# Cross-attention block on one core: the planner's order of TensorE, ScalarE and VectorE is replaced by written strings

## What is computed

```
q = (layer_norm(x) * g + b) @ Wq + bq        # 16 heads of 16
k, v = ctx @ Wk + bk, ctx @ Wv + bv
attn = softmax(q @ k.T / 4)                  # 512 x 1601 for each head
y = x + (attn @ v) @ Wo + bo
out = y + silu(layer_norm(y) @ W1 + b1) @ W2 + b2      # FF = 1024
```

## Time and profile before

| what | us |
|---|---|
| median of three runs | 3663.59 |
| the profiled execution | 3659.6 |
| its span | 3657.8 |
| prologue, until the first quarter's scores | 96 |
| batch 0 / each of batches 1 to 14 / batch 15 | 202.2 / 222.3 / 192.1 |
| busy in a middle batch: TensorE / VectorE / ScalarE / GpSimd | 216.5 / 153.4 / 140.2 / 58.7 |

### The profile page before, as it was taken

One profiled execution on the slowest core, in us unless ns is written; L12 is line 12 of the kernel. 1 busy time (PEld: TensorE's weight loads), 2 busy tenths in 40 slices (PEclk: granted clock), 3 DMA queues, 4 the chain that ended last, 5 costly groups with the idle time before them and its releaser, 6 DMA issues.

```text
span 3657.8 us, 52477 instructions
## 1 busy us (share of the span) xinstructions
PE 3495.7 (96%) x19620; PEld 1552.4 (42%) x19620; DVE 2474.9 (68%) x4580; ACT 2243.8 (61%) x2979; POOL 950.3 (26%) x1340
## 2 busy tenths in 40 slices
PE   6899999999999999999999999999999999999997
PEld 2333444444444444443444444444444444434434
DVE  6767667676676767667676676766767676676761
ACT  2566666666666665666656666566666656666564
POOL 5122223121231322323222241212313223132202
PEclk8999999999999999999999999999999999999999
DMA  4223212132221222212232121321213222122200
GB/s 97 60 40 63 40 33 46 34 66 42 36 49 32 59 42 52 41 30 52 42 66 40 29 48 35 66 43 33 50 32 61 43 44 49 30 53 42 43 7 12
DMA packets 121535, 162.96 MB, mean 45 GB/s; under 512 B 37040, under 2 KB 102592, under 8 KB 118208
## 3 DMA queue, kind: packets, MB, share of 16 engines
q1 hardware_dynamic: 120896, 159.40, 22.2%
q10 hardware_dynamic: 384, 0.20, 0.0%
HBM read 46.43 MB, written 8.39 MB: 15 GB/s over the span
## 4 chain that ended last, share of the span: by engine, by line
PE 81%; DVE 12%; ACT 3%; issue 2%; DMA 1%; SPq 0%; POOL 0%; ACTq 0%; DVEq 0%
PE o_ps L1197 20%; PE rows_ps L1163 19%; PE scores L1178 14%; DVE chunk_max L974 8%; PE side L1131 6%; PE side L1128 6%; PE side L1117 5%; PE side L1109 5%; ACT probs L821 2%; PE side L1113 1%; PE side L1121 1%; DVE stats L852 1%; DVE resid L879 1%; PE side L1100 1%; ACT ctxT L738 1%
## 5 line engine op out<-in xcount | busy, mean ns | idle before, releaser
L974 DVE TENSOR_REDUCE chunk_max<-rows_ps 128x1 f32<-128x512 f32 (+1 forms) x3328 | 2117.2, 666 | 1049.8 <-PE rows_ps L1163 1041.5
L821 ACT ACTIVATE probs<-scores 128x1024 f32<-128x1024 f32 (+1 forms) x1664 | 1676.9, 1024 | 1135.3 <-PE scores L1178 1128.3
L1163 PE MATMUL rows_ps<-k_stack,q_stack 96*128 96x512 bf16 (+1 forms) x4096 | 1215.7, 338 | 83.9 <-DVE chunk_max L974 52.4
L1178 PE MATMUL scores<-q_stack,k_stack 99*128 99x512 bf16 (+1 forms) x3328 | 1036.5, 379 | 7.2 <-DMA q_stack<-shift_parts 4.2
L1197 PE MATMUL o_ps<-probs,v_sb 128*32 128x512 f32 x6656 | 886.3, 605 | 0.4 <-ACT probs L821 0.4
L1163 PEld LDWEIGHTS rows_ps<-k_stack,q_stack 96*128 96x128 bf16 x4096 | 332.0, 97 | 1169.9 <-DVE chunk_max L974 960.9
L1178 PEld LDWEIGHTS scores<-q_stack,k_stack 99*128 99x128 bf16 (+1 forms) x3328 | 324.8, 100 | 303.7 <-issue 42.0
L585 POOL TENSOR_TENSOR rest<-whole,k_parts 128x512 f32<-128x512 f32 x124 | 117.1, 944 | 962.8 <-ACT k_parts L766 928.3
L1128 PE MATMUL side<-hT,w_sb 128*128 128x256 f32 x968 | 258.6, 379 | 0.0
L1197 PEld LDWEIGHTS o_ps<-probs,v_sb 128*32 128x32 f32 x6656 | 130.8, 108 | 294.3 <-issue 220.4
L1131 PE MATMUL side<-w_sb,ffT 128*128 128x256 f32 x960 | 244.9, 381 | 0.6
(11 more groups left out here) (126 smaller groups left out, 2054.0 us busy)
## 6 DMA issues: line engine op xcount, KB each, us to landing
k_stack<-k_parts SPq DMA_DIRECT2D x768, 50.0 KB, 2.2
k_stack<-k_stack SPq DMA_DIRECT2D x192, 200.1 KB, 5.6
ctx_nat<-in_ctx SPq DMA_DIRECT2D x47, 512.0 KB, 4.0
q_stack<-q_stack SPq DMA_DIRECT2D x192, 64.0 KB, 3.4
q_stack<-q_parts SPq DMA_DIRECT2D x756, 16.0 KB, 1.8
x_nat<-in_x SPq DMA_DIRECT2D x16, 512.0 KB, 6.1
resid<-in_x SPq DMA_DIRECT2D x32, 256.0 KB, 2.7
out<-resid SPq DMA_DIRECT2D x32, 256.0 KB, 2.5
```

Source lines behind the costliest of these rows:

```text
L821: nc.scalar.activation(probs[0:rows, (q + t) % 2, 2 * LQ * pair:2 * LQ * (pair + 1)], scores[0:rows, 2 * LQ * pair:2 * LQ * (pair + 1)], A ...
L974: nc.vector.tensor_reduce(dst, src, AX.X, ALU.max).then_inc(rows_read, 1)
L1163: last = nc.tensor.matmul(rows_ps[:, m % 2, d0:d0 + w], q_stack[s][0:STACK, h, P * t:P * (t + 1)], k_stack[s][0:STACK, h, k0:k0 + w], star ...
L1178: ins = nc.tensor.matmul(scores[0:keys_in(t), LQ * j:LQ * (j + 1)], k_stack[s][:, h, P * t:P * t + keys_in(t)], q_stack[s][:, h, :], start ...
```

## The change

The tables and `plan` are removed. `BOTH` lists only the sequence of side steps of each quarter (the same steps in the same quarters and sequence), and three tables of strings set the order: TENSOR (s, m, d, p as above), SCALAR (e an exponential, r the read of a side step, c the copy of `o_ps`), VECTOR (m a maxima read, i inversion, n negation, x and b moments, a the addition of wo, y of w2, g `finish_silu`). In the first and the last batch the letters of missing steps are skipped. The reads of the maxima, the exponentials and all waits are the same code as before. The first twelve slots of the opening quarter do two maxima each. "pp" is new: two PV tiles one after the other.

The turn's matmul gets all 128 columns: `neg_parts` is widened with zeros, and ScalarE still copies 12 partitions. For k and q ScalarE reads the bank once into `whole`, waits for that, and copies the first part from `whole` (semaphore `first_parts` tells GpSimd). For w1 it reads each half once, waits, and takes one tanh over 512 columns from `ffT` (semaphore `tanh_made` tells VectorE).

```diff
+TENSOR = (
+    "spmssmdsmdddmssmdddmdsmpsmmddddsmssmddddmsmpddmmssddddmddmpmmsddmsssmdmdmssssmppssmsmsddssmmpmmssssm"
+    "pmssmddddmssmssmpmmsddmsmddmssssppmmssddddmssmpmmddmsmsssmddmpm",
+    "ssmpdmdddssmssmddddmsmsddddpsdsdmmddpmssmddddmssmssmpmddmddssmssmdpdmmssdddmmsssdsmpmmpmssmdmsmdmsmp"
+    "mmdmdsmmsssdmmdmssmssdmdpmsddddsmpssddddmmpddddssmmssdmssmdssmmppmmss",
+    "dssdmdddmpmmdddsssmsmdddddmsmddsdssmmppmssmdssddmmddssdddmmppddmssssmdmddmdmssssmmddddmmssppmmssddmd"
+    "dddmmssssdddmmdddppmmssddmddssmmssddddmpmssmssddmmddpsssmsmddmssmddsmmpddddsmmspsmm",
+    "dmdmmssssdmmdssmpmmdsmsdmmpdsdmmssspmmssdmsmsssdmmppmmsssdmsdmssmddsmsmppmmsssdsmmdssddmmppssmmssddm"
+    "ddmdsddmssmspmmddddsmmdddddsssmmpmddddssssmmpmssmssmpmm",
+)
+SCALAR = (
+    "ceereereeereeeeereeeeeereeeereeeer",
+    "ecrerereerereererreeereerereererererereeeree",
+    "ecreeereeeerreereereeeeeeereereeerree",
+    "reerceerreeeereeeereeeereeeeeereeee",
+)
+VECTOR = (
+    "mmmmmmmimmmmmmimmmmmmmmmambmbbmmmmmmmmmmmmmmmmnmammmmmmmmbmbmbmg",
+    "mmmmimmxmmmmmmmxmmmmxmmimmmmmmmmmmmmmmmmmmmmmnmmmmgmmmmmmmm",
+    "mmmmmmmmmmmmmmmmmmmmmmmgmmigmmmmmmimmmmymmmmmnmmmmmmgmmmmgmm",
+    "mmmmmmmmmimmmmmmmmmimmmmmmmmmmmgmmgmmmmmmmmnmmmymmmmmmmmmm",
+)
...
-        neg_parts = sb("neg_parts", [P, QT, PARTS, 4], BF16)
+        neg_parts = sb("neg_parts", [P, QT, P // 4, 4], BF16)
...
-                    ins = nc.tensor.matmul(side[0:4 * PARTS, P * i:P * (i + 1)],
+                    ins = nc.tensor.matmul(side[:, P * i:P * (i + 1)],
...
-                    nc.scalar.activation(whole[:, n % 2, 0:w], src[:, 0:w], ACT.Identity, bias=bias, scale=scale)
-                    last = nc.scalar.activation(parts[:, 0, off:off + w], src[:, 0:w], ACT.Identity, bias=bias,
-                                                scale=scale)
+                    nc.scalar.activation(whole[:, n % 2, 0:w], src[:, 0:w], ACT.Identity, bias=bias, scale=scale)\
+                        .then_inc(side_read, 1)
+
+                    act.wait_ge(side_read, step_value(start, k))
+                    nc.scalar.copy(parts[:, 0, off:off + w], whole[:, n % 2, 0:w]).then_inc(first_parts, 1)
+                    return
...
+                    for half in range(2):
+                        m = 2 * m2 + half
+                        last = nc.scalar.activation(ffT[:, m, :], src[:, QH * half:QH * (half + 1)], ACT.Identity,
+                                                    bias=half_b1[:, m:m + 1], scale=0.5)
+                    last.then_inc(side_read, 1)
+
+                    act.wait_ge(side_read, step_value(start, k))
...
-                    last = halves_step(src, kind, arg, ffT, tanh_sb, hT)
+                    nc.scalar.activation(tanh_sb[:, :], ffT[:, 2 * m2:2 * m2 + 2, :].rearrange("p m q -> p (m q)"),
+                                         ACT.Tanh).then_inc(tanh_made, 1)
```

More of the change, by code:

```diff
@@ L73, in tiles_in @@
     return range(4 * c, min(4 * c + 4, KT))
[L78 to L84, removed]
+FINISHING = ("wo", "h", "w1", "w2")
@@ new lines, with kept @@
+SCALAR = (
[8 more added lines that the diff above has]
+    "mmmmmmmmmmmmmmmmmmmmmmmgmmigmmmmmmimmmmymmmmmnmmmmmmgmmmmgmm",
+    "mmmmmmmmmimmmmmmmmmmimmmmmmmmmmmgmmgmmmmmmmmnmmymmmmmmmmmm",
+)
+def kept(q, keep):
+    return [step for step in BOTH[q] if keep(step[0])]
@@ L104 @@
+FIRST = tuple(kept(q, lambda kind: kind not in FINISHING) for q in range(4))
+LAST_BATCH = (BOTH[0],) + tuple(kept(q, lambda kind: kind in FINISHING + ("turn",)) for q in (1, 2)) \
+    + (kept(3, lambda kind: kind in FINISHING),)
 PER_BATCH = sum(map(len, BOTH))
@@ L145, in products, with side_products, chosen @@
     return [(i, j) for i in range(first) for j in range(second)]
-def products_at(steps, u):
+def side_products(q, steps):
     found = []
[L151 to L155, removed]
-    return found
+    for step in BOTH[q]:
+        todo = products(*step)
+        for n, product in enumerate(todo):
+            found.append((steps.index(step),) + step + (product, n, n == len(todo) - 1) if step in steps else None)
+    return found
+def chosen(q, steps, kinds):
+    return [(steps.index(step),) + step if step in steps else None for step in BOTH[q] if step[0] in kinds]
 M_ROWS = QT * 4
@@ L184, in maxima @@
     return b + (q + ahead) // 4, (q + ahead) % 4, m
[L188 to L212, removed]
 def wait(eng, sem, value):
@@ L671, in quarter @@
             def quarter(b, q, start, steps):
-                kinds = [step[2:] for step in steps]
+                kinds = steps
                 ahead, s = PREPARED[q]
                 if q == 3:
-                    splits(b + ahead, s, start, steps)
+                    splits(b + ahead, s, steps)
                 if q > 0:
@@ L807, in quarter @@
                 ahead, s = PREPARED[q]
[L808 to L811, removed]
+                unit, reads = iter(range(UNITS)), iter(chosen(q, steps, ("v", "ctx", "k", "q", "x", "turn", "h", "w1")))
+                for what in SCALAR[q]:
+                    if what == "c":
                         if q > 0:
                             copy_group(b, q - 1)
-                        elif not (isinstance(b, int) and b == 0):
+                        elif b > 0:
                             copy_group(b - 1, 3)
[L817 to L828, removed]
+                    elif what == "r":
+                        read = next(reads)
+                        if read:
+                            k, kind, arg = read
+                            if kind in FINISHING:
+                                side_step(b - 1, None, start, k, kind, arg)
+                            else:
+                                side_step(b + ahead, s, start, k, kind, arg)
+                    else:
+                        exponentials(b, q, next(unit))
             def epilogue(start):
@@ L1011, in quarter @@
             def quarter(b, q, start, steps):
-                first, last = (isinstance(b, int) and b == n for n in (0, B - 1))
                 bm, qm = (b, q + 1) if q < 3 else (b + 1, 0)
[L1014 to L1027, removed]
-                            sum_moments(b - 1, start, k, arg, u - end)
-                    for slot in slots[1:]:
-                        read_rows(*maxima(b, q, slot))
-                    if u == M_END - 1 and not (last and q == 3):
-                        negate_maxima(bm, qm)
-                    for k, kind, arg in at(steps, u):
-                        if kind in ("wo", "w2"):
-                            add_step(b - 1, start, k, kind, arg)
-                        if kind == "wo":
-                            sum_moments(b - 1, start, k, arg, 0)
```

141 lines of the change are left out of this document (91 added, 50 removed).

## The result

The changed kernel takes 3473.15 us (median of 4 runs, 3470.28 to 3475.45) against 3663.83 us; the ratio of the times is 0.948 (95% interval 0.947 to 0.949). The forecast was 3484. The profiled execution of the changed kernel took 3472.1 us, with a span of 3470.3.

What follows compares the result with a forecast made beforehand. Bound: TensorE's own work plus 12.9 us of waits a middle batch. Terms 9.5 + 2.0 + 0.8 = 12.3 us, times 14, plus about 8, took 180 us off: 3480, or 3484 on the runs' scale; 8-in-10 range 3446 to 3540.

Steps and rivals of the forecast that it cites:

- The maxima's places: TensorE's maxima products: slots closer than 1.17 us to the one two before are spread out, 9.5 us a batch gained.
- the weight loads that wait for chunk_max: Sign in a batch's waits: rows_ps weight loads waiting for chunk_max fall to a third of 57.7 us or less.
- PV tiles side by side: TensorE's ten adjacent PV tile pairs a batch save 0.19 to 0.23 us each, taken as 2.0 us a batch.
- The full-width turn: The turn's product at 128 columns instead of 12 loses both steps around it: 4 x 0.19 = 0.8 us a batch.
- One pass over the side bank: ScalarE's reads for k, q and w1: earlier bank release worth 0 to 1 us a batch, within the 9.5.
- What is late next: SyncE's transfers: stack has 5 us cover at slot 40, shift 5.1 us, third context chunk 5.2 us against 4.0.
- Sum: Whole kernel: 12.3 us less a middle batch, 172 for 14, about 8 in the end batches, 180 us in all.
- A: Rival: half of TensorE's waits come back as fixed orders stall the maxima's reads; 133 us gained, 3531; chance 0.19.
- B: Rival: only the tiling mode switches go, all waits return elsewhere; 44 us gained, 3620; chance 0.06.
- E: Rival: the change does nothing, TensorE being bound by its own products alone; 3664; chance 0.01.
- C: Rival: all TensorE's waits go and merges pay 0.23 us; 236 us gained, 3428; chance 0.10.
- D: Rival: slower, VectorE's list blocks itself when other groups come up before their input; 104 us lost, 3768; chance 0.04.

Runs made afterwards that it cites:

- e7: The changed kernel with sixteen maxima products of a batch moved ahead, closer to the slot two before: 3527.70 us, ratio 0.963.
- e2: The changed kernel with the old order written as strings for all three engines, keeping the full-width turn and one pass: 3653.57 us, ratio 0.997.
- e5: The changed kernel with the ten adjacent PV tiles of a batch moved apart by one letter: 3499.75 us, ratio 0.955.
- e9: e1 with the turn's product of 12 columns again: 3458.23 us, ratio 0.943.
- e1: The changed kernel with the next batch's first two context chunks and x asked for sooner, in quarter 3: 3454.64 us, ratio 0.943.
- e4: The changed kernel with ScalarE's two bank reads for k and q and four for w1, as before: 3490.35 us, ratio 0.953.
- e11: e1 with the eight finish_silu of a batch up to three letters sooner in VectorE's strings: 3574.67 us, ratio 0.975.
- e3: The changed kernel with the turn's product of 12 columns again: 3465.37 us, ratio 0.946.
- e8: e1 with quarter 0's shift placed ahead of the second group's q parts and repeats, which move behind the turn: 3571.55 us, ratio 0.975.

## Why the prediction was right

*The maxima's places.* The term was 9.5 us a batch and a middle batch at 210.0 us. A clean batch is 208.1, the mean 209.55: the waits fell by 11.5 us, and 1.4 of that were given back to the context chunk: 10.1 against 9.5. The count of two-slot distances was the right instrument: its 8.2 us of shortfall are gone, e7 puts 4.7 back and gets 4.7, e2 keeps the old order and with it all but 0.2 us of its waits. The residue of 3.4 us was kept for what stays or comes late; in a clean batch 1.4 are there, on the mean 2.8. Of the signs named in advance the length of a middle batch holds, but one is missed: the weight loads that wait for chunk_max are at 27.7 us, not at a third of 57.7 or less. That row was a poor measure of the cost; the idle matmuls fell from 2.3 us to 0.4.

*PV tiles side by side.* 2.0 predicted, 2.4 measured (e5). I had allowed 0.04 us for the starts of the records; a pair and the step behind it take 1.95 where two single tiles take 2.20, so nothing of the 0.04 is there, and the steps ahead and behind are saved whole.

*The full-width turn.* 0.8 predicted, 0.27 measured (e9). The direction was right, the size was not: I took all four turns as four times the one of the earlier trace rows. On the old order that is nearly so (0.65, e2). But the new order puts two of them right behind a PV tile, where a narrow product costs no step of its own (the timelines of e1 and e9 above). The term belonged to the order it was put into, not to the one it was read from.

*One pass over the side bank.* Priced within the waits at 0 to 1 us; on the old order it is 0.2 of e2's 0.8 us a batch, on the new one its undoing costs 1.6 (e4). This is where "hidden" was too simple: whether a release is hidden depends on the order around it, and the new order was laid close behind it.

*What is late next.* Here a step failed. I followed the stack fill only to its first user, slot 40, where the cover of 5 us held, and not to the end of SyncE's queue. The stacks' issues alone take 46 us, in a quarter that is 48 us long (its first scores at 713.74, the next quarter's at 761.76), with the shift and three loads behind them; the 3.7 us that were free there before, outside of the earlier trace rows, are gone. The first context chunk was the transfer that became late, while I looked at the third. Price: 18.5 us of the gain (e1). The shift's cover of 5.1 us was also too coarse: it was read from the full strings, and in batch 15, where letters drop out, the last quarter's first score stands 2.2 us behind the turn and waits (below).

*Sum.* 14 middle batches: 14 x 12.8 = 179 against 172. The ends: by the distances between turns batch 0 gained 1.6 us and batch 15 up to its last turn 9.9; from there to the end 3.0 were lost. There TensorE waits 1.84 us for the shift, where it waited 0.40 before, and then 0.7 for an exponential, and the clock stands at 0.50 for the next 5 us, where it was 1.00:

```profile
3372.51 1.04 PE L1199 MATMUL scores<-q_stack,k_stack 99*128 99x512 bf16 x4 [1.84 <-DMA q_stack<-shift_parts]
```

8.5 against 8. In all 187.5 us of 3657.8, against 180. That the total lies so close owes something to luck: without the late chunk, which no term named, it would have been 3455, 29 us below the forecast instead of 11, though inside the range.

*The rivals.* A (half of the waits return) and B (all do) are refuted by the 1.4 us that are left, and E by the result. C (all go) was nearer than I thought: e1, where only 1.4 us of waits are left in a clean batch, is at 3454.6. D is refuted for this string and shown as a mechanism by e11.

## What to carry to other kernels

Where two banks pass between a producer and a reader, measure the time from a product to its bank being free again, and write the order so that no two slots of the same bank are closer; a count over the written order gave the price to a tenth of a microsecond a batch (e7). When a stretch gets shorter, lay every queue's issues of that stretch end to end, not only up to the first user: the one that fills the stretch is what comes next, and what stands last in it is what will be late. Give work its place in an engine's list by when its input is made: up to three places sooner cost 120 us here (e11); later wasn't tried.

## What had not been expected of the hardware

Behind the wait of 1.3 us at 763 us in the changed kernel the granted clock of the stretch from 765 to 769 us was 0.59, with scores 0.43 us apart instead of 0.22, the lower of its two levels (1.2 GHz), for about 3 us. Thus in that batch, of 211.0 us, the late chunk cost 2.9 us where the wait alone was 1.3. The length of the wait doesn't settle whether the clock falls. In the changed kernel it fell behind all five waits for the chunk of 1.27 to 2.00 us and behind none of four of 0.68 to 0.96; in e3 it stayed at 1.00 behind waits of 1.27 and 1.36. In e11, which has the same wait of 2.75 us in each middle batch, it fell behind 11 of them and stayed behind three, and there the same pair of PV tiles takes 1.92 us instead of 3.58 in the timeline's rows. In e8 it fell behind all 14 waits of 4.7 to 6.0 us. What else it depends on can't be told from these runs.

A product of 12 columns behind a PV tile of 32 costs no step ahead of it, while the same product among products of 128 columns costs 0.19 us (e2, e9).
